# One window of destination rows for two neighbouring quads of edges

## The chip, the cores and the metric

The kernel runs on 1 core of one Trainium2 chip. The metric is the device time of one execution in microseconds (us). The engines are called by their short names: PE (TensorE), DVE (VectorE), ACT (ScalarE), POOL (GpSimd) and SP (SyncE).

## What is computed

Four graph layers run one after the other over 3125 nodes of 128 features and 53125 edges that are sorted by their destination. The change touches the first layer alone, and in it the sum over edges:

```
h = relu(layernorm(x))
msg_in = concatenate([h[src], h[dst], edge_attr])          # 128 + 128 + 2 columns
msgs = relu(msg_in @ mW1 + mb1) @ mW2 + mb2
agg = segment_sum(msgs, dst) / max(count(dst), 1)
upd = relu(concatenate([h, agg]) @ uW1 + ub1) @ uW2 + ub2 + h
x = x + layernorm(upd) * gamma + beta
```

Layers 1 to 3 are x + f(relu(layernorm(x))), where f sums the neighbours' rows (plain, weighted, or scaled by degree). The kernel does these sums as dense products with blocks of a matrix of edge counts or weights.

## The kernel before

**The sweep.** The edges are cut into 104 quads of 512 edges (NQ = 104, four chunks of 128 edges in each). One loop over the quads, called the sweep here, takes roughly from 57 us to 631 us of the profiled span. It makes the sums of layer 0 and, beside them, the count and weight blocks that the later layers use. The order of work is written out by hand, as a list of instructions and semaphore waits for each engine; nothing is scheduled by a program. For quad q:

- POOL gathers the 512 rows of the table P = h @ mW1[0:128] by the sources, as four indirect DMAs (`rows_at`, L766) into one of six buffers G. It may run six quads ahead of PE's use.
- PE makes the messages before their relu in `pre(q)`: for each chunk the identity times G (L1694) and a one-hot matrix of rows `sT` times `Qr` (L1695). `Qr` is the window of q: 125 rows of h @ mW1[128:256] from row first(q), with the two rows for the edge attributes and the bias below them. The window is one product in `q_window` on PE (L1681) into PSUM and one copy in `q_window` on DVE (L1260) to SBUF.
- ACT takes the relu (L903). PE sums the messages of the four chunks by destination in `seg(q)` (L1708), with one-hot matrices that DVE makes in `onehot` (L1266), into 128 columns of PSUM bank 2 or 3, by turns. DVE adds these to the running sums ST in `add(q)` (L1253).
- For the later layers DVE makes the operands of a step of blocks (`block_operands`, L1277, L1280, L1284), PE multiplies them in two halves, `blocks(u, 0)` and `blocks(u, 1)` (L1726, L1728), and ACT reads them (`read_blocks`, L928 and L934). Here u = q - 4.

PE's order in the loop at quad q is: pre(q + 1), blocks(u, 0), seg(q), q_window(q + 4), a piece if there is one, blocks(u, 1). ACT's is: relu(q + 1) (L903), `window_rows(q + 2)` (L916), the read of blocks(u, 0), `rows_off(q + 3)` (L909), the read of the piece of quad q - 1, the read of blocks(u, 1), normalization steps. DVE's is: add(q - 1), the window copy q + 3, the read of an A piece, onehot(q + 1), block operands, normalization steps.

**The pieces.** Where the sums of two node tiles are complete, the node update of layer 0 is done within the sweep. There are 11 such pieces g, and SLOT gives each three quads: A at 57 + 4g (sums times mW2, read by DVE, L1354), U at 59 + 4g (L1748 and L1749, relu read by ACT, L944) and V at 62 + 4g (L1755 and L1756, read by ACT, L948). The product of a piece goes into columns 256 to 511 of bank 2 or 3 (`slot_bank`), the windows into the columns between, so one bank holds a quad's sums, windows and pieces. An engine may write a bank only when no other reads it. `seg(n)` therefore waits on `s_add`, on `s_Qr` (windows copied), and on `ev[...]` for the read of the piece of slot n - 2.

After the sweep come the last piece, the layer norms of the last rows, and the dense products (L1855, L1870), which keep PE busy to the end.

Of the kernel before, what the change touches and what calls it, by code (L numbers as in the profile page):

```python
# [5 lines left out]
def gnn_kernel(nc, x_in, src_in, dst_in, ea_in, ew_in, mW1, mb1, mW2, mb2, uW1, ub1, uW2, ub2,  # L6
# [30 lines left out]
    def first(q):  # L37
        return max(0, 30 * q + (q >> 3) - 47)
# [14 lines left out]
    assert STEPS + LAG == NQ  # L53

# [8 lines left out]
    def complete(t):  # L63

        return min(q for q in range(NQ) if q + 1 == NQ or first(q + 1) >= 128 * (t + 1))
# [27 lines left out]
    with ctx:  # L93
# [95 lines left out]
        GS, QS, TS, RS, OS, OUTS, SETS = 6, 6, 4, 3, 3, 4, 3  # L189
        LEAD = 4  # L190
# [246 lines left out]
        def slot_bank(q):  # L437
            return bank(2 + q % 2)[:, 256:512]
# [408 lines left out]
        def _(act):  # L847
# [272 lines left out]
        def _(dve):  # L1120
# [47 lines left out]
            link(dve.scalar_tensor_tensor(sq[:, :], pio[:, :], 30.0, sq[:, :], ALU.mult, ALU.add))  # L1168
            link(dve.tensor_scalar(sq[:, :], sq[:, :], -47.0, 0.0, ALU.add, ALU.max))
# [70 lines left out]
            def add(q):  # L1240
                if q in SLOT:
                    name, g = SLOT[q]
                    dve.wait_ge(mm[name], g + 1)
                elif q + LEAD < NQ:
                    dve.wait_ge(s_Qmm, q + LEAD + 1)
                else:
                    dve.wait_ge(s_seg, q + 1)
                if q == 0:
                    dve.wait_ge(s_zero, 1)
                else:  # L1250
                    dve.wait_ge(s_add, q)
                at = first(q)
                dve.tensor_tensor(ST[:, at:at + 128], ST[:, at:at + 128], bank(2 + q % 2, 128), ALU.add)\  # L1253
                    .then_inc(s_add, 1)

            def q_window(n):
                dve.wait_ge(s_Qmm, max(n + 1, LEAD))
                if n >= QS:
                    dve.wait_ge(s_pre, n - QS + 1)
                dve.tensor_copy(Qr[0:WIN, n % QS, :], q_bank(n)[0:WIN, :]).then_inc(s_Qr, 1)  # L1260
# [129 lines left out]
            for n in range(LEAD):  # L1390
# [245 lines left out]
        def _(pe):  # L1636
# [42 lines left out]
            def q_window(n):  # L1679
                at = first(n)  # L1680
                pe.matmul(q_bank(n), hT[:, at:at + 128], w_m1[:, 1, :], start=True, stop=True).then_inc(s_Qmm, 1)  # L1681

            def pre(n):
# [5 lines left out]
                pe.wait_ge(s_Qr, n + 1)  # L1689
                if n >= 2:  # L1690
                    pe.wait_ge(s_R, n - 1)
                for c in range(4):
                    to = bank(n % 2)[:, 128 * c:128 * c + 128]
                    pe.matmul(to, ident[:, :], G[:, n % GS, c, :], start=True, stop=False)  # L1694
                    last = pe.matmul(to, sT[:, n % TS, 128 * c:128 * c + 128], Qr[:, n % QS, :], start=False, stop=True)  # L1695
                last.then_inc(s_pre, 1)

            def seg(n):
                pe.wait_ge(s_R, n + 1)
                pe.wait_ge(s_oh, n + 1)  # L1700
                if n >= 2:
                    pe.wait_ge(s_add, n - 1)
                pe.wait_ge(s_Qr, min(max(n - 1, 0) + LEAD, NQ))
                if n - 2 in SLOT:
                    name, g = SLOT[n - 2]
                    pe.wait_ge(ev[name], g + 1)
                for c in range(4):
                    last = pe.matmul(bank(2 + n % 2, 128), R[:, n % RS, c, :], oh[:, n % OS, c, :],  # L1708
                                     start=c == 0, stop=c == 3)
                last.then_inc(s_seg, 1)  # L1710
# [27 lines left out]
            def piece_A(g, to):  # L1738
                ts = PIECES[g]
                pe.wait_ge(s_add, complete(ts[-1]) + 1)  # L1740
# [21 lines left out]
            for n in range(LEAD):  # L1762
                q_window(n)
            pre(0)
            for q in range(NQ):
# [19 lines left out]
                if q + LEAD < NQ:  # L1785
                    q_window(q + LEAD)
# [114 lines left out]
            pe.wait_ge(s_add, NQ)  # L1901
# [101 lines left out]
```

## Time and profile before

| what | value |
|---|---|
| time, 3 runs | 1059.24 us median, 1053.53 to 1059.82 |
| span of the profiled execution, first to last instruction | 958.9 us |
| median less span (launch and end, outside the span) | 100.3 us |
| PE busy | 853.5 us (89%) |
| DVE busy | 639.7 us (67%) |
| POOL busy | 518.0 us (54%) |
| ACT busy | 509.8 us (53%) |

The profile shows one execution, and the times do not say which of the three it is. A time is therefore compared with 958.9 us plus the 100.3 us that lie outside the span. Busy shares are means over stages with different limits. Register, branch and semaphore instructions and the issue of DMAs don't count as busy, so POOL's 0.3 us between two gathers is idle time in these numbers.

### The profile page before, as it was taken

What the parts mean: (1) busy time and instruction counts of PE and PEld (TensorE: products, weight loads), DVE (VectorE), ACT (ScalarE), POOL (GpSimd) and SP (SyncE); (2) the same over time, 40 slices, a digit from 0 to 9 for tenths busy, and PEclk for the clock granted to TensorE, in tenths of its full rate; (3) what the DMA queues carried; (4) which work ended last, traced back from release to release, by engine and by line L of the source; (5) the groups of instructions that cost most, each with busy time, mean ns of one, the idle gap of its engine ahead of it and who ended that gap; (6) DMA issues with size and microseconds to landing.
All of it is one profiled execution on the core that took longest, in us unless ns stands there. A gap on an engine that the chain in (4) does not pass through costs nothing.

```text
span 958.9 us, 20995 instructions
## 1 busy us (share of the span) xinstructions
PE 853.5 (89%) x7785; PEld 783.6 (82%) x7785; DVE 639.7 (67%) x1766; ACT 509.8 (53%) x1029; POOL 518.0 (54%) x477
## 2 busy tenths in 40 slices
PE   2445988888998788999999999998999999999997
PEld 2345978888998788899998999977889888888886
DVE  7607998787877877688888889858653311115664
ACT  3413765655766556677777777843443011114863
POOL 4177777777777877777777777753110000023110
PEclk9767999999999999999999999999999999999999
DMA  5672656556765586666566666664246888884500
GB/s 153 179 176 63 180 166 177 161 171 193 209 183 166 155 148 200 170 171 182 165 184 166 172 183 167 176 194 146 69 154 232 317 287 300 299 287 144 161 23 25
DMA packets 117410, 169.14 MB, mean 176 GB/s; under 512 B 17287, under 2 KB 83485, under 8 KB 117306
## 3 DMA queue, kind: packets, MB, share of 16 engines
q1 hardware_dynamic: 99834, 137.67, 45.0%
q0 software_dynamic: 13872, 28.32, 13.4%
q10 hardware_dynamic: 3600, 1.77, 0.6%
q8 instruction: 64, 1.05, 0.5%
q14 instruction: 40, 0.33, 0.1%
HBM read 109.26 MB, written 58.45 MB: 175 GB/s over the span
## 4 chain that ended last, share of the span: by engine, by line
PE 40%; POOL 34%; issue 10%; DMA 10%; DVE 3%; ACT 2%; SPq 1%; ACTq 0%; DVEq 0%
POOL room L766 33%; PE ps L1870 14%; PE ps L1855 14%; DMA room<-p_rows,idx 7%; PE ps L1694 3%; DMA edge_windows<-room 3%; PE ps L1695 2%; PE ps L1839 2%; PE ps L1728 1%; PE ps L1708 1%; PE ps L1639 1%; ACT h L872 1%; POOL pair L766 1%; DMA ST<-in_src 1%; PE ps L1668 1%
## 5 line engine op out<-in xcount | busy, mean ns | idle before, releaser
L766 POOL DMA_INDIRECT room<-p_rows,idx x416 | 440.4, 1059 | 144.6 <-issue 120.1
L1694 PE MATMUL ps<-room,ident 128*128 128x128 f32 x832 | 175.1, 293 | 61.7 <-DMA room<-p_rows,idx 60.1
L1694 PEld LDWEIGHTS ps<-room,ident 128*128 128x128 f32 x832 | 130.9, 198 | 70.7 <-DMA room<-p_rows,idx 50.9
L1728 PE MATMUL ps<-room 128*128 128x100 bf16 x2400 | 169.3, 207 | 0.0
L1695 PE MATMUL ps<-room 128*128 128x128 f32 x832 | 166.0, 282 | 0.0
L1284 DVE TENSOR_TENSOR room<-room,Wp 128x800 bf16<-128x800 bf16 x300 | 155.4, 572 | 0.0
L903 ACT ACTIVATE g<-ps 128x512 f32<-128x512 f32 x104 | 62.2, 598 | 170.9 <-PE ps L1695 169.4
L1726 PE MATMUL ps<-room 128*128 128x100 bf16 x800 | 151.7, 208 | 0.0
L1728 PEld LDWEIGHTS ps<-room 128*128 128x128 bf16 x2400 | 147.9, 97 | 3.5
L1870 PE MATMUL ps<-room,h 128*128 128x256 f32 (+1 forms) x650 | 136.2, 371 | 0.0
L1870 PEld LDWEIGHTS ps<-room,h 128*128 128x128 f32 x650 | 119.2, 190 | 15.2
L1695 PEld LDWEIGHTS ps<-room 128*128 128x128 f32 x832 | 131.3, 199 | 0.0
L1855 PE MATMUL ps<-wide_room,parts 128*128 128x512 f32 (+1 forms) x520 | 116.7, 378 | 0.0
L1708 PE MATMUL ps<-g 128*128 128x128 f32 x832 | 116.1, 282 | 0.0
L928 ACT ACTIVATE room<-ps 128x400 uint8<-128x400 f32 x200 | 100.1, 501 | 27.8 <-PE ps L1726 26.8
L1855 PEld LDWEIGHTS ps<-wide_room,parts 128*128 128x128 f32 x520 | 91.3, 189 | 19.5 <-DVE parts L1370 0.3
L1708 PEld LDWEIGHTS ps<-g 128*128 128x128 f32 x832 | 100.8, 191 | 0.0
L934 ACT ACTIVATE room<-ps 128x400 f32<-128x400 f32 x200 | 100.7, 503 | 0.0
L1253 DVE TENSOR_TENSOR ST<-ST,ps 128x128 f32<-128x128 f32 x104 | 29.3, 282 | 104.0 <-PE ps L1681 67.4
L1266 DVE TENSOR_SCALAR g<-iota,dstT 128x128 f32<-128x128 f32 x416 | 92.1, 299 | 0.0
L864 ACT ACTIVATE sd<-mv,eps 128x2 f32<-128x2 f32 (+3 forms) x45 | 13.5, 301 | 138.0 <-DVE mv L1143 136.5
L1726 PEld LDWEIGHTS ps<-room 128*128 128x128 bf16 x800 | 78.4, 98 | 3.9 <-issue 3.6
(193 smaller groups left out, 1137.3 us busy)
## 6 DMA issues: line engine op xcount, KB each, us to landing
weight_blocks<-room SPq DMA_DIRECT2D x100, 400.0 KB
room<-weight_blocks SPq DMA_DIRECT2D x12, 3200.0 KB
room<-dst_row SPq DMA_DIRECT2D x104, 128.0 KB
room<-count_blocks SPq DMA_DIRECT2D x8, 1600.0 KB
count_blocks<-room SPq DMA_DIRECT2D x100, 100.0 KB
room<-p_rows,idx POOLq DMA_INDIRECT x416
first_c<-count_blocks SPq DMA_DIRECT2D x4, 1600.0 KB
edge_windows<-room SPq DMA_DIRECT2D x1, 3328.0 KB
```

Of the source, the lines that this page charges most:

```text
L766: return pool.indirect_dma_start(to, None, table, bass.IndirectOffsetOnAxis(ap=at, axis=0))
L928: act.activation(cnt_out[:, u % OUTS, :, at16].rearrange("p h (b w) -> p b h w", w=4), of, ACT.Copy)\
L934: act.activation(w_out[:, u % OUTS, :, at16].rearrange("p h (b w) -> p b h w", w=4), of, ACT.Copy)\
L1266: last = dve.tensor_scalar(oh[:, q % OS, c, :], iota[:, :], dstT[:, q, c:c + 1], None, ALU.is_equal)
L1284: last = dve.tensor_tensor(movw[:, k, a, :, :, :], mov[:, k, :, :, :], blocks_of(Wp[:, a, :], u, KCOLS), ALU.mult)
L1694: pe.matmul(to, ident[:, :], G[:, n % GS, c, :], start=True, stop=False)
L1695: last = pe.matmul(to, sT[:, n % TS, 128 * c:128 * c + 128], Qr[:, n % QS, :], start=False, stop=True)
L1708: last = pe.matmul(bank(2 + n % 2, 128), R[:, n % RS, c, :], oh[:, n % OS, c, :], start=c == 0, stop=c == 3)
L1726: counted = pe.matmul(bank(4 + hh)[:, at], lo, mov[:, k, i, :, t], start=True, stop=True)
L1728: weighed = pe.matmul(bank(6 + hh)[:, at], lo, movw[:, k, a, i, :, t], start=a == 0, stop=a == PARTS - 1)
L1855: last = pe.matmul(to, Hr[:, t, a, :], at[:, k, 0:n], start=a == 0 and t == 0, stop=a == 1 and t == NT - 1)
L1870: last = pe.matmul(bank(dense_bank(j))[:, 256 * half:256 * half + 32 * c], h[:, t, :], ring_w[(2 * j + half) % 3][:, 0:c, t, :], start=t = ...
```

## The change

Quads 2m and 2m + 1 form a pair. Both use the same first row: first(q) is max(0, 30 (q & ~1) + (q >> 3) - 32) where it was max(0, 30 q + (q >> 3) - 47). So there is one window product and one copy for a pair (52 instead of 104, two pairs ahead, 4 buffers Qr for pairs instead of 6 for quads), and seg(2m) and seg(2m + 1) accumulate into the same 128 columns, from which DVE adds once for a pair. The banks alternate by pairs. A window is written after seg of an even quad, into the bank that the pair does not use; ahead of it stands the new wait `other_bank_free(n)`, on the add of the pair before and, if quad n - 1 was the slot of a piece, on the read of that piece. seg(n) keeps its waits on windows and pieces for even n alone.

```diff
     def first(q):
-        return max(0, 30 * q + (q >> 3) - 47)
+        return max(0, 30 * (q & ~1) + (q >> 3) - 32)
...
         def q_bank(n):
-            at = 256 if 2 <= n < LEAD else 128
-            return bank(2 + n % 2)[:, at:at + 128]
+            return bank(2 + (n + 1) % 2)[:, 128:256]
...
         def slot_bank(q):
-            return bank(2 + q % 2)[:, 256:512]
+
+            m = q // 2 if q % 2 else q // 2 + 1
+            return bank(2 + m % 2)[:, 256:512]
...
@@ ACT, read_slot
-                act.wait_ge(s_add, q + 1)
-                if q + LEAD < NQ:
-                    act.wait_ge(s_Qr, q + LEAD + 1)
+                if q % 2:
+                    act.wait_ge(s_add, q // 2 + 1)
+                elif q // 2 + AHEAD < NH:
+                    act.wait_ge(s_Qr, q // 2 + AHEAD + 1)
...
@@ DVE, the loop
                 if q >= 1:
-                    add(q - 1)
-                    if q - 1 + LEAD < NQ:
-                        q_window(q - 1 + LEAD)
+                    if (q - 1) % 2:
+                        add(q // 2 - 1)
+                    elif q // 2 + AHEAD < NH:
+                        q_window(q // 2 + AHEAD)
...
@@ PE
             def seg(n):
+                m = n // 2
                 pe.wait_ge(s_R, n + 1)
                 pe.wait_ge(s_oh, n + 1)
-                if n >= 2:
-                    pe.wait_ge(s_add, n - 1)
-                pe.wait_ge(s_Qr, min(max(n - 1, 0) + LEAD, NQ))
-                if n - 2 in SLOT:
-                    name, g = SLOT[n - 2]
+                if n % 2 == 0:
+                    pe.wait_ge(s_Qr, min(m + AHEAD, NH))
+                    if n - 2 in SLOT:
+                        name, g = SLOT[n - 2]
+                        pe.wait_ge(ev[name], g + 1)
+                for c in range(4):
+                    last = pe.matmul(bank(2 + m % 2, 128), R[:, n % RS, c, :], oh[:, n % OS, c, :],
+                                     start=n % 2 == 0 and c == 0, stop=n % 2 == 1 and c == 3)
+                last.then_inc(s_seg, 1)
+
+            def other_bank_free(n):
+
+                pe.wait_ge(s_add, n // 2)
+                if n - 1 in SLOT:
+                    name, g = SLOT[n - 1]
                     pe.wait_ge(ev[name], g + 1)
...
                 seg(q)
-                if q + LEAD < NQ:
-                    q_window(q + LEAD)
+                if q % 2 == 0:
+                    if q >= 2:
+                        other_bank_free(q)
+                    else:
+                        pe.wait_ge(s_Qr, AHEAD)
+                    if q // 2 + AHEAD < NH:
+                        q_window(q // 2 + AHEAD)
```

The other hunks adapt counts to this (the semaphore values of `add`, `pre` and `piece_A`, one more small instruction on DVE that makes first(q) for every partition, two rows of constants less to load for each Qr buffer that is gone).

PE at quad 68, the quad after slot U of piece 2, before: seg (L1708), window (L1681), second half of the blocks. Names after "waits" are semaphores.

```order
L1708 MATMUL ps<-g3 128x128 [waits q_window_ready,quad_added,V_read,onehot_ready,messages_ready]
L1708 MATMUL ps<-g3 128x128 x3
L1681 MATMUL ps<-w_m1,hT 128x128
L1726 MATMUL ps<-room 128x100 [waits weights_read,counts_read]
L1728 MATMUL ps<-room 128x100 x3
```

The same place after the change (seg is L1718 there, the window L1691):

```order
L1718 MATMUL ps<-g3 128x128 [waits q_window_ready,V_read,onehot_ready,messages_ready]
L1718 MATMUL ps<-g3 128x128 x3
L1691 MATMUL ps<-w_m1,hT 128x128 [waits U_read,quad_added]
L1743 MATMUL ps<-room 128x100 [waits weights_read,counts_read]
L1745 MATMUL ps<-room 128x100 x3
```

The wait for the reading of the U piece has moved from seg of quad 69 (not shown) to the window of quad 68, and the wait for the add from ahead of seg to behind it.

ACT at the same quad, before: relu, window rows, the blocks' first half, rows off, the read of the U piece (L944).

```order
L903 ACTIVATE g3<-ps 128x512 [waits quad_in_psum,messages_in_psum]
L916 ACTIVATE room<-room,onesr 125x512 [waits messages_in_psum,rows_off_ready]
L928 ACTIVATE room<-ps 128x4x25x4 [waits counts_stored_0,counts_in_psum]
L934 ACTIVATE room<-ps 128x4x25x4 [waits weights_stored_0,weights_in_psum]
L909 ACTIVATE room<-room,npio 125x512 [waits dst_spread_3]
L944 ACTIVATE ST<-ps,cols 128x256 [waits U_done,q_window_ready,quad_added]
```

And after:

```order
L906 ACTIVATE g3<-ps 128x512 [waits quad_in_psum,messages_in_psum]
L919 ACTIVATE room<-room,onesr 125x512 [waits messages_in_psum,rows_off_ready]
L931 ACTIVATE room<-ps 128x4x25x4 [waits counts_stored_0,counts_in_psum]
L937 ACTIVATE room<-ps 128x4x25x4 [waits weights_stored_0,weights_in_psum]
L912 ACTIVATE room<-room,npio 125x512 [waits dst_spread_3]
L947 ACTIVATE ST<-ps,cols 128x256 [waits U_done,quad_added]
```

Nothing moved on ACT; one wait of the read of the piece is gone.

## Rows read from the trace of the kernel before

**Rows 1.** Waits over the whole span: us in total, times, longest.

```profile
POOL room L766 <- issue: 120.1, 394, 0.3
...
PE ps L1694 <- DMA room<-p_rows,idx: 60.1, 43, 17.7
...
POOL room L766 <- PE ps L1695: 6.4, 21, 0.3
```

**Rows 2.** Waits between 400 and 626 us.

```profile
POOL room L766 <- issue: 47.0, 154, 0.3
...
PE ps L1694 <- DMA room<-p_rows,idx: 7.7, 10, 1.6
```

**Rows 3.** Source view of the gathers L766: duration min/median/max in ns, first and last start.

```profile
L766 POOL DMA_INDIRECT room<-p_rows,idx x416: 939/947/4158, 45.2 to 619.9; - x139
```

**Rows 4.** Timeline at 439 us, POOL and DVE: start, us, engine, line.

```profile
439.21 0.95 POOL L766 DMA_INDIRECT room<-p_rows,idx  x1 [0.30 <-issue]
439.24 0.29 DVE L1253 TENSOR_TENSOR ST<-ST,ps 128x128 f32<-128x128 f32 x1 [0.89 <-PE ps L1749]
439.44 0.28 DVE L1260 COPY room<-ps 125x128 f32<-125x128 f32 x1
440.43 0.56 DVE L1277 TENSOR_TENSOR room<-iota_k,Kt 128x800 bf16<-128x800 bf16 x1
440.46 1.35 POOL L766 DMA_INDIRECT room<-p_rows,idx  x1 [0.30 <-issue]
```

**Rows 5.** Timeline of PE at quad 68.

```profile
443.30 0.39 PE L1681 MATMUL ps<-w_m,hT 128*128 128x128 f32 x2
443.53 0.21 PE L1726 MATMUL ps<-room 128*128 128x100 bf16 x1
```

**Rows 6.** Timeline of ACT at quad 68.

```profile
441.82 0.60 ACT L903 ACTIVATE g<-ps 128x512 f32<-128x512 f32 x1 [0.33 <-PE ps L1695]
...
444.31 0.48 ACT L944 ACTIVATE ST<-ps,cols 128x256 f32<-128x256 f32 x1
```

**Rows 7.** Timeline at quad 96, the last but one of its kind.

```profile
595.75 0.39 PE L1681 MATMUL ps<-w_m,hT 128*128 128x128 f32 x2
...
596.75 0.48 ACT L944 ACTIVATE ST<-ps,cols 128x256 f32<-128x256 f32 x1
```

**Rows 8.** PE's first and last wait of [rows 2], of ten.

```profile
402.05 0.49 PE L1694 MATMUL ps<-room,ident 128*128 128x128 f32 x2 [0.96 <-DMA room<-p_rows,idx]
...
624.42 0.49 PE L1694 MATMUL ps<-room,ident 128*128 128x128 f32 x2 [1.59 <-DMA room<-p_rows,idx]
```

**Rows 9.** DVE's read of an A piece (quad 74), PE's window.

```profile
472.74 0.41 DVE L1354 TENSOR_TENSOR room<-ps,room 128x256 f32<-128x256 f32 x1
...
476.51 0.39 PE L1681 MATMUL ps<-w_m,hT 128*128 128x128 f32 x2
```

**Rows 10.** Timeline at quad 4, PE and DVE, and the next wait of PE for a gather.

```profile
97.35 0.39 PE L1681 MATMUL ps<-w_m,hT 128*128 128x128 f32 x2
98.63 0.27 DVE L1253 TENSOR_TENSOR ST<-ST,ps 128x128 f32<-128x128 f32 x1
...
122.71 0.49 PE L1694 MATMUL ps<-room,ident 128*128 128x128 f32 x2 [1.81 <-DMA room<-p_rows,idx]
```

**Rows 11.** Chain that ended last, 619 to 642 us: start, us, what.

```profile
619.92 4.45 DMA room<-p_rows,idx
...
641.71 0.49 ACT h L948
```

**Rows 12.** PE after a longer wait; windows (the third number from the end is the granted clock).

```profile
237.17 0.49 PE L1694 MATMUL ps<-room,ident 128*128 128x128 f32 x2 [1.98 <-DMA room<-p_rows,idx]
...
238.00:240.00 2.00, 2.00 (x12) 2.00 (x11) 0.48 (x1) 0.00 (x0) 1.39 (x3) 0.50 1.10 344
240.00:242.00 2.00, 2.00 (x24) 1.94 (x24) 0.00 (x0) 1.38 (x3) 1.70 (x2) 0.75 1.11 366
...
124.00:126.00 2.00, 2.00 (x29) 1.99 (x29) 2.00 (x5) 1.21 (x3) 1.59 (x2) 1.00 0.68 151
```

More of the change, by code:

```diff
@@ L53, in gnn_kernel @@
     assert STEPS + LAG == NQ
+    NH = NQ // 2
+    AHEAD = 2
+    assert NQ == 2 * NH
     PIECES = [[t, t + 1] for t in range(0, NT - 3, 2)] + [list(range(NT - 3, NT))]
@@ L63, in complete @@
     def complete(t):
-        return min(q for q in range(NQ) if q + 1 == NQ or first(q + 1) >= 128 * (t + 1))
+        return min(q for q in range(1, NQ, 2) if q + 1 == NQ or first(q + 1) >= 128 * (t + 1))
     SLOT = {}
@@ L1167, in _ @@
             link(dve.tensor_copy(sq[:, :], q8_i[:, :]))
-            link(dve.scalar_tensor_tensor(sq[:, :], pio[:, :], 30.0, sq[:, :], ALU.mult, ALU.add))
-            link(dve.tensor_scalar(sq[:, :], sq[:, :], -47.0, 0.0, ALU.add, ALU.max))
+            link(dve.tensor_single_scalar(q8_i[:, :], pio_i[:, :], 126, ALU.bitwise_and))
+            link(dve.scalar_tensor_tensor(sq[:, :], q8_i[:, :], 30.0, sq[:, :], ALU.mult, ALU.add))
+            link(dve.tensor_scalar(sq[:, :], sq[:, :], -32.0, 0.0, ALU.add, ALU.max))
             dve.wait_ge(s_dst, 48)
@@ L1238, in _, with add @@
             dve.memset(ST[:, :], 0.0).then_inc(s_zero, 1)
-            def add(q):
+            def add(m):
+                q = 2 * m + 1
                 if q in SLOT:
@@ L1388, in piece_steps @@
                         stage(g)
-            for n in range(LEAD):
+            for n in range(AHEAD):
                 q_window(n)
@@ L1679, in q_window @@
             def q_window(n):
-                at = first(n)
+                at = first(2 * n)
                 pe.matmul(q_bank(n), hT[:, at:at + 128], w_m1[:, 1, :], start=True, stop=True).then_inc(s_Qmm, 1)
@@ L1688, in pre @@
                 pe.wait_ge(s_sT, n + 1)
-                pe.wait_ge(s_Qr, n + 1)
+                pe.wait_ge(s_Qr, n // 2 + 1)
                 if n >= 2:
@@ L1694, in pre @@
                     pe.matmul(to, ident[:, :], G[:, n % GS, c, :], start=True, stop=False)
-                    last = pe.matmul(to, sT[:, n % TS, 128 * c:128 * c + 128], Qr[:, n % QS, :], start=False, stop=True)
+                    last = pe.matmul(to, sT[:, n % TS, 128 * c:128 * c + 128], Qr[:, n // 2 % QS, :], start=False, stop=True)
                 last.then_inc(s_pre, 1)
             def seg(n):
+                m = n // 2
                 pe.wait_ge(s_R, n + 1)
                 pe.wait_ge(s_oh, n + 1)
-                if n >= 2:
-                    pe.wait_ge(s_add, n - 1)
-                pe.wait_ge(s_Qr, min(max(n - 1, 0) + LEAD, NQ))
-                if n - 2 in SLOT:
-                    name, g = SLOT[n - 2]
+                if n % 2 == 0:
[11 more added lines that the diff above has]
+                    name, g = SLOT[n - 1]
                     pe.wait_ge(ev[name], g + 1)
[L1707 to L1710, printed above, removed]
             def blocks(u, hh):
@@ L1739, in piece_A @@
                 ts = PIECES[g]
-                pe.wait_ge(s_add, complete(ts[-1]) + 1)
+                pe.wait_ge(s_add, complete(ts[-1]) // 2 + 1)
                 pe.wait_ge(s_ld[g % RING], 32 * (g // 3 + 1))
@@ L1761, in _ @@
             pe.wait_ge(s_edE, 2)
-            for n in range(LEAD):
+            for n in range(AHEAD):
                 q_window(n)
@@ L1784, in _ @@
                 seg(q)
-                if q + LEAD < NQ:
-                    q_window(q + LEAD)
+                if q % 2 == 0:
+                    if q >= 2:
+                        other_bank_free(q)
+                    else:
+                        pe.wait_ge(s_Qr, AHEAD)
+                    if q // 2 + AHEAD < NH:
+                        q_window(q // 2 + AHEAD)
                 if q in SLOT:
@@ L1900, in _ @@
             dense_group(1, 0)
-            pe.wait_ge(s_add, NQ)
+            pe.wait_ge(s_add, NH)
             pe.wait_ge(ev["V"], IN_SWEEP)
```

19 lines of the change are left out of this document (10 added, 9 removed).

## The prediction

> **What bounds the kernel now.** The totals mislead here. PE is busy for 89% of the span, but in the sweep it waits for POOL. I read the waits first. Over the whole span POOL's idle time before a gather is almost all "issue", 0.3 us at a time, and its waits for PE's `pre` are never longer than that same 0.3 us [rows 1]: POOL never waits for a free buffer once the gathers run. A gather takes 0.947 us at the median [rows 3] and 0.30 us lies between two, so four gathers, a quad, cost at least 5.0 us, and the 416 of them set the sweep's pace. PE on the other hand has waited 60.1 us for gathered rows [rows 1].
>
> The reader is then to see how this changes along the sweep. Between 400 and 626 us, where the pieces are made, PE's waits for gathers sum to only 7.7 us in ten waits [rows 2], of 0.96 us at the first and 1.59 us at the last [rows 8], while POOL goes on without a pause. There PE and POOL are nearly even: POOL is ahead by 7.7 us in 226, 3.4%. Whatever is taken from PE gains nothing; whatever is added to it costs nothing up to those 7.7 us, and after that the whole amount. At the end the chain goes from the last gather (619.92) through its landing into PE at 624.42 and on, without a wait for another engine, to ACT at 641.71 [rows 11]. So how late PE is at its last gather arrives in full at the end.
>
> **The windows and adds that go.** 52 of 104 window products leave PE. One costs PE 0.23 us, from the window's start at 443.30 to the next product at 443.53 [rows 5]. That is 12.0 us over the sweep, but up to quad 59 it only lengthens PE's waits for gathers. DVE loses 52 adds (0.29 us) and 52 copies (0.28 us) [rows 4], 30 us in all. DVE is not what POOL or, in steady state, PE waits for, so this is worth nothing by itself. Could a lighter DVE speed the gathers? A gather that runs beside an add and a copy takes 0.95 us, the median; one that starts beside the block operands L1277 takes 1.35 us [rows 4]. What slows gathers is left as it was. I take 0 for it. The bound on the good side is that each of the 52 adds and copies held up a gather for its whole length, 30 us, which the 0.95 us speaks against.
>
> **The new waits on the add.** After seg(2m) PE now waits for add(m - 1), which DVE does at the head of its turn 2m. Before the change PE needed DVE one turn less far. In steady state DVE stands ready early. It is late only at the start, behind the unpacking of the windows: at quad 4 the add of quad 3 ends at 98.63 + 0.27 = 98.90, and PE is through seg at 97.35 [rows 10], so PE would wait 1.6 us; the same at quad 6 is some 0.4 us. Behind the waiting window on PE stand the second half of the blocks and the next `pre`. POOL is several quads ahead at this point and has six buffers, and PE's next wait for a gather at 122.71 is 1.81 us long [rows 10]. Together with DVE's shorter turns that covers it: 0, and if the cover failed, 2 us in a stretch that is followed by 280 us in which POOL is ahead.
>
> **The new waits on pieces.** A slot's read was waited for by seg two quads later. Now it is waited for one quad later, by the window (or, from quad 100 on, by the blocks behind it). For A pieces this is free: DVE starts its read at 472.74 and needs 0.41 us, and PE comes to the window of that quad only at 476.51 [rows 9]. V pieces stand at even quads and keep their wait. For U pieces it is not free. ACT starts its turn with the relu at 441.82, just after PE's `pre` of the same turn, and comes to L944 only after four other instructions, at 444.31; it ends at 444.79 [rows 6]. PE is through seg at 443.30 [rows 5]. PE now stands for 444.79 - 443.30 = 1.49 us and a few hundredths for the semaphore, say 1.53 us. Both engines start from the same product, so this is the same each time: at quad 96 it is 596.75 + 0.48 - 595.75 = 1.48 us [rows 7]. ACT doesn't start earlier after the change, since its order is the same and its start hangs on PE. There are 11 U pieces (slots 59 to 99), so 16.8 us are added to PE between 400 us and the end. Queued behind the wait are the window, the blocks' second half and the next `pre`, for which ACT and DVE then wait in turn; DVE's copy of the window comes 1.5 us later and its add in the next turn stood idle for longer than a microsecond, so DVE absorbs this.
>
> **The sum.** From quad 60 on, PE gains 16.8 us of standing and loses 20 of 40 windows, 4.6 us: 12.2 us more. 7.7 us of its waits for gathers take up the first part. A wait can only take up lateness that is there when it comes; the first stall, at 400 us, precedes the first wait of 0.96 us, and each group of four quads then adds 1.53 - 2 x 0.23 = 1.07 us of lateness against some 0.7 us of waiting (7.7 / 11), so all 7.7 us are used. PE is late at its last gather by 12.2 - 7.7 = 4.5 us. This goes through the chain to the end. 958.9 + 4.5 = 963.4 us of span, and with the 100.3 us outside it 1063.7 us, or 0.4% more than the median of 1059.24. Lateness of 4.5 us is less than one quad of the six that POOL may run ahead, so POOL is not held up.
>
> **Rivals.** *Not slower: the stalls are hidden.* If PE's own pace had more room than its waits show (waits under 0.3 us are not in the list), or if DVE's shorter turns and a steadier PE bring ACT's turn forward, up to the whole of 4.5 us disappears. Some 0.4 us more room for each group of four quads is enough. POOL alone then sets the end, 1059 us. For it speaks that PE and POOL are so nearly even that small errors decide; against it that the 1.48 us repeats to the hundredth in [rows 5 to 7].
>
> *Slower by much: the clock drops at the stalls.* After PE's wait of 1.98 us the granted clock stood at 0.50 for 2 us and at 0.75 for 2 us more [rows 12], the lower of its two levels (1.2 GHz of 2.4) for part of the time; that lost 1.0 + 0.5 = 1.5 us. After the wait of 1.81 us at 122.71 it stayed at 1.00 [rows 10, 12]. A stall of 1.5 us lies just under these. If it decided the clock each time, 11 x 1.5 = 16.5 us would come on top: 1080 us. [...] The Trainium skill ("TensorE: Matmul & The Clock Gate", section "Why this matters for your kernels") would allow idle gaps longer than any of these before the clock falls back; by it this rival has no ground. The trace disagrees, with a drop after 1.98 us, so I keep it.
>
> *The gathers change their pace.* What a gather loses to DVE's block operands depends on how the two fall together; 1.35 against 0.95 us is 0.4 us for an unlucky one [rows 4]. DVE's turns are now 0.29 us shorter, so all meetings shift. One gather in each quad that meets or misses would be 0.4 x 50 = 20 us over the first 50 quads at the most, either way; a tenth to a third of the meetings is what I would expect, 2 to 6 us: 1058 to 1070 us. Once PE is the bound, from quad 64 or so, a faster POOL gains nothing. The Trainium skill ("SBUF — State Buffer", section on who interferes with whom) says that VectorE instructions in a two-port mode hold a port that GpSimd needs to write descriptors. Were the window's copy one of these, as the page says of fp32 copies within SBUF, its removal would give up to 52 x 0.28 = 15 us; the 0.95 us beside it speaks against that.
>
> *The change doesn't do what it says.* If some quad's destinations fell outside 125 rows, the kernel would redo everything in its slow branch, for milliseconds. A pair covers some 60 rows of destinations plus the drift, so 65 are left. 1%.
>
> **How the numbers follow.** Chances: forecast (1061 to 1067) 0.55; stalls hidden 0.15; pace of the gathers, 0.08 for faster (1045 to 1058) and 0.11 for slower (1067 to 1075) than the others give; clock 0.08 (1080); anything else 0.03. The range of 1054 to 1073 leaves out the clock and the ends of the pace. One per cent is 10.6 us, about what a measurement of this kernel can tell from no change: the three runs before lie 6.3 us apart. Within 1% (1048.6 to 1069.8) lie the forecast, the hidden stalls and most of the pace: 0.80. Slower by more: the clock and part of the pace, 0.15. Faster by more: 0.05.
>
> **What the profile after should show.** PE waits of 1.4 to 1.6 us at the window L1691 for ACT L947, ten of them, and one more at the blocks of quad 100. PE's waits for gathers after 405 us gone or nearly so, and the last `pre` starting about 4 us after its gather has landed, at about 629 us. POOL's gathers unchanged, 416 with a median of 0.947 us and the last one at about 620 us. 52 each of L1257, L1269 and L1691. Up to 400 us more waiting of PE for gathers, by about the windows that went. If the last gather itself ends earlier or later by more than 3 us, the pace has changed and the sum is made from a wrong base. If PE still waits for its last gather, the stalls were hidden. If the granted clock after 400 us falls below 1.00, it is the clock.

## The result and the profile after

The changed kernel takes 1086.15 us at the median of four runs (1084.93 to 1091.63), the kernel before 1059.53 us at the median of four (1053.53 to 1062.10): a ratio of 1.0278, with a 95% interval of 1.0245 to 1.0311. It is slower by 27 us where 4.5 us were forecast, outside the range and on the side that got 0.15.

The profiled execution took 1086.68 us and its span is 1082.7 us. So only 4 us lie outside the span, where [rows 1 to 12] came from an execution with a span 100 us under the time. The waits over the whole span, in the order us in total, times, longest:

```profile
POOL room L769 <- issue: 99.4, 325, 0.4
...
POOL room L769 <- PE ps L1705: 81.9, 40, 5.4
...
POOL room L769 <- remote: 65.7, 50, 2.4
...
PE ps L1745 <- issue: 45.2, 82, 1.2
```

This is not the kernel of [rows 1]. POOL, which waited for PE 0.3 us at a time there, now waits 5.4 us at the longest, and PE stands 82 times at the products of the weight blocks (L1745) without any semaphore. PE's stalls at the window L1691 behind the U slots 59, 63 and so on are all there; four of the ten and the one at quad 100 from PE's timeline:

```profile
467.93 0.77 PE L1691 MATMUL ps<-w_m,hT 128*128 128x128 f32 x2 [2.57 <-issue]
...
551.82 0.56 PE L1691 MATMUL ps<-w_m,hT 128*128 128x128 f32 x2 [3.03 <-ACT ST L947]
...
607.26 0.77 PE L1691 MATMUL ps<-w_m,hT 128*128 128x128 f32 x2 [3.19 <-issue]
...
719.06 0.55 PE L1691 MATMUL ps<-w_m,hT 128*128 128x128 f32 x2 [3.17 <-ACT ST L947]
...
742.74 0.21 PE L1743 MATMUL ps<-room 128*128 128x100 bf16 x1 [1.42 <-issue]
```

The ten last 30.1 us together (2.44 to 3.21 each), twice what was forecast. PE's last product of counts in the turn before the stall at 719.06, and ACT up to that stall:

```profile
711.09 0.20 PE L1743 MATMUL ps<-room 128*128 128x100 bf16 x1
...
714.40 0.51 ACT L931 ACTIVATE room<-ps 128x400 uint8<-128x400 f32 x1 [2.37 <-remote]
714.80 0.50 ACT L937 ACTIVATE room<-ps 128x400 f32<-128x400 f32 x1
715.19 0.87 ACT L875 ACTIVATE h<-x,nb,rs 128x128 f32<-128x128 f32 x2
715.96 0.59 ACT L906 ACTIVATE g<-ps 128x512 f32<-128x512 f32 x1
...
718.43 0.49 ACT L947 ACTIVATE ST<-ps,cols 128x256 f32<-128x256 f32 x1
```

From the start of the relu to the end of the U read ACT needs 718.43 + 0.49 - 715.96 = 2.96 us, as in [rows 6], where it is 2.97. What differs is where the relu stands against PE. PE's `seg` ended at 719.06 - 3.17 = 715.89, so the relu starts with the end of `seg`; in [rows 5, 6] it started 1.48 us ahead of it. Ahead of the relu stands ACT's read of the blocks, held for 2.37 us. What it waits for is PE's product of 711.09, which ends at 711.30; the trace also has the times at which semaphores are incremented, by which one engine tells another that an instruction is done (no line above prints them), and the increment of this product arrives only at 714.38.

The stall does not end in PE. POOL's gathers around the one at 607.26:

```profile
603.05 0.99 POOL L769 DMA_INDIRECT room<-p_rows,idx  x1 [1.38 <-PE ps L1705]
604.35 0.94 POOL L769 DMA_INDIRECT room<-p_rows,idx  x1 [0.30 <-issue]
605.59 0.94 POOL L769 DMA_INDIRECT room<-p_rows,idx  x1 [0.30 <-issue]
606.84 0.95 POOL L769 DMA_INDIRECT room<-p_rows,idx  x1 [0.30 <-issue]
613.18 0.94 POOL L769 DMA_INDIRECT room<-p_rows,idx  x1 [5.40 <-PE ps L1705]
```

POOL waits for PE in every quad, 1.4 us, and 5.40 us in the one behind the stall: here the gathers start some 4 us later than their pace asks. The stall itself was 3.19 us. From the first gather of quad 66 to that of quad 103, nine of POOL's steps from quad to quad lie behind a stall and take 82.7 us; the others take 6.21 us each, so a stall cost 3.0 us at the mean. How that comes about is told under "Why the prediction was wrong".

### The profile page after: what moved, and what is told of

It is laid out like the page before. It is cut to its first block, busy times and chain, and to the rows that moved or that the text cites. A ratio compares the mean times of both kernels' runs of the same rounds, so it can differ in the third digit from the quotient of the medians.

```text
span 1082.7 us, 20507 instructions
## 1 busy us (share of the span) xinstructions
PE 887.9 (82%) x7681; PEld 796.8 (74%) x7681; DVE 631.5 (58%) x1663; ACT 514.3 (48%) x1029; POOL 499.2 (46%) x477
## 4 chain that ended last, share of the span: by engine, by line
PE 78%; issue 12%; ACT 3%; DVE 3%; another core or an unknown queue 1%; DMA 1%; POOL 1%; SPq 0%; ACTq 0%; DVEq 0%
PE ps L1892 12%; PE ps L1745 12%; PE ps L1877 12%; PE ps L1704 10%; PE ps L1718 10%; PE ps L1705 9%; PE ps L1743 4%; PE ps L1861 2%; PE ps L1691 2%; ACT h L875 1%; DMA room<-p_rows,idx 1%; PE ps L1649 1%; PE ps L1760 1%; POOL room L769 1%
## 5 line engine op out<-in xcount | busy, mean ns | idle before, releaser
L769 POOL DMA_INDIRECT room<-p_rows,idx x416 | 421.7, 1014 | 258.5 <-issue 99.4
L1745 PE MATMUL ps<-room 128*128 128x100 bf16 x2400 | 194.2, 211 | 47.2 <-issue 45.2
L1704 PE MATMUL ps<-room,ident 128*128 128x128 f32 x832 | 179.0, 299 | 37.9 <-DMA room<-p_rows,idx 16.3
L1745 PEld LDWEIGHTS ps<-room 128*128 128x128 bf16 x2400 | 155.7, 100 | 62.2 <-issue 57.7
L1705 PE MATMUL ps<-room 128*128 128x128 f32 x832 | 171.0, 289 | 0.1
L1743 PE MATMUL ps<-room 128*128 128x100 bf16 x800 | 157.9, 212 | 12.4 <-issue 12.1
L1704 PEld LDWEIGHTS ps<-room,ident 128*128 128x128 f32 x832 | 136.8, 206 | 42.2 <-issue 39.0
L1718 PE MATMUL ps<-g 128*128 128x128 f32 x832 | 125.9, 287 | 16.5 <-issue 15.5
L1705 PEld LDWEIGHTS ps<-room 128*128 128x128 f32 x832 | 136.0, 206 | 0.0
L1286 DVE TENSOR_TENSOR room<-iota_k,Kt 128x800 bf16<-128x800 bf16 x100 | 57.4, 574 | 133.0 <-remote 128.0
L1718 PEld LDWEIGHTS ps<-g 128*128 128x128 f32 x832 | 105.6, 193 | 24.2 <-issue 23.8
L1743 PEld LDWEIGHTS ps<-room 128*128 128x128 bf16 x800 | 80.4, 101 | 20.4 <-issue 19.9
```

Of the source, the lines that this page charges most:

```text
L769: return pool.indirect_dma_start(to, None, table, bass.IndirectOffsetOnAxis(ap=at, axis=0))
L1718: last = pe.matmul(bank(2 + m % 2, 128), R[:, n % RS, c, :], oh[:, n % OS, c, :], start=n % 2 == 0 and c == 0, stop=n % 2 == 1 and c == 3)
L1743: counted = pe.matmul(bank(4 + hh)[:, at], lo, mov[:, k, i, :, t], start=True, stop=True)
L1745: weighed = pe.matmul(bank(6 + hh)[:, at], lo, movw[:, k, a, i, :, t], start=a == 0, stop=a == PARTS - 1)
```

## The experiments

Times of the same kernel differ from one set of runs to the next (before: 1059 and 1072 us, and on one chip 1071.54 and later 1058.53), so each kernel is set against the runs of before in its own set.

**The kernel before once more, and the ranges alone.** *b_same* is the unchanged kernel; *p1_range* has only `first(q)` and `complete(t)` of the change:

```diff
-        return max(0, 30 * q + (q >> 3) - 47)
+        return max(0, 30 * (q & ~1) + (q >> 3) - 32)
```

> The kernel before, unchanged, profiled again beside the changed one. The page of before has a span of 958.9 us against a time of 1059 us, the page of after 1082.7 us against 1086 us. If the profiled execution of before was one in an unusual state (theory A), this span is near 1055 us, 4 us below its time, with PE standing without a semaphore ('issue') in the sweep as in the profile after. If the change itself brought these stalls (theory B), the span is 959 us again, without them, and 100 us lie outside it.

> One part alone: the row ranges of the pairs (both quads of a pair use the same first row), but with a window product, a copy and an add for every quad as before. It computes the same output. Every theory that blames waits, windows or adds expects the time of before, 1059 us within 5. If the ranges themselves cost (consecutive adds to the same columns of ST, or pieces becoming complete later), it goes towards 1086 us.

One run each, beside 1071.54 us of before: 1075.62 us (span 1073.8) and 1073.85 us (span 1072.0). The ranges cost nothing that one run can show. *b_same* is as theory A had it: the span is near the time, and PE stands without a semaphore in the kernel before too. Its waits over the whole span:

```profile
ACT room L928 <- remote: 235.6, 90, 5.8
...
POOL room L766 <- remote: 77.6, 50, 5.7
PE ps L1728 <- issue: 68.7, 129, 1.2
POOL room L766 <- PE ps L1695: 68.0, 40, 4.8
...
PE ps L1694 <- DMA room<-p_rows,idx: 19.0, 1, 19.0
```

The unchanged kernel waits for a gather once, at the start, where [rows 1] has 43 such waits and 60.1 us. It is POOL that waits for PE. From quad 8 to 44 a quad lasts 6.255 us between ACT's relus, against 5.342 in the execution of [rows 1 to 12]. Every later trace has a span within 4 us of the time and stands of PE in the sweep (short ones in *e4_gathers*): [rows 1 to 12] describe an execution that the timed ones are not. Why that one ran otherwise no run shows. Its timeline at 301 us, PE, ACT and POOL:

```profile
300.92 0.39 PE L1695 MATMUL ps<-room 128*128 128x128 f32 x2
...
301.31 1.15 POOL L766 DMA_INDIRECT room<-p_rows,idx  x1 [0.30 <-issue]
...
302.55 0.21 PE L1728 MATMUL ps<-room 128*128 128x100 bf16 x1 [0.50 <-issue]
...
303.27 0.21 PE L1726 MATMUL ps<-room 128*128 128x100 bf16 x1 [0.52 <-issue]
...
303.32 0.51 ACT L928 ACTIVATE room<-ps 128x400 uint8<-128x400 f32 x1 [2.86 <-remote]
...
303.76 0.94 POOL L766 DMA_INDIRECT room<-p_rows,idx  x1 [1.30 <-remote]
```

Once per quad PE slows down or stops inside the blocks, with no semaphore to wait for. The last gather ahead of POOL's pause ends at 301.31 + 1.15 = 302.46, PE is at full pace again at 303.27, 0.81 us later, and ACT and POOL are released behind it. From 200 to 630 us POOL pauses for over 0.6 us 63 times; in 58 of them PE's last resumption within the pause lies 0.79 to 1.04 us behind the gather's end.

The times of the increments say what is held. POOL's gather at 303.76 waits for PE's `pre`, whose last product ends at 301.31. Its increment arrives at 303.51. At the median of 59 quads from 200 to 600 us it arrives 2.13 us behind the end of `pre` and 1.25 us behind the end of POOL's last gather, and POOL goes on 0.26 us later. In the same stretch the increments of ACT and DVE arrive 0.01 us behind their instructions. So do all 95 recorded ones of PE after 770 us, where no gather runs, and all of PE in the execution of [rows 1 to 12]. PE's work is thus not what POOL waits for, as far as its recorded ends go (they are modelled): PE has room, 2 us in most quads and 1 to 2 us from quad 64 on, where the pieces are.

**The wait for the U read alone, and three versions without it.** *e2_wait* is the kernel before with only the moved wait:

```diff
                 seg(q)
+                if SLOT.get(q - 1, " ")[0] == "U":
+                    pe.wait_ge(ev["U"], SLOT[q - 1][1] + 1)
                 if q + LEAD < NQ:
```

> The kernel before with one thing added: PE's window of the quad after each U slot waits until ACT has read the U piece, as in the changed kernel. The output is the same. T1: 11 stalls of about 3 us, 30 us or more slower than before (1085 to 1095). T2: at most the 4.5 us that the prediction worked out, about 1064 us.

*e1_defer* is the changed kernel, with the window behind a U slot, its wait and its copy one quad later:

```diff
-                if q % 2 == 0:
+                if q % 2 == 0 and not after_U(q):
...
+                if after_U(q - 1):
+                    other_bank_free(q - 1)
+                    if q // 2 + AHEAD < NH:
+                        q_window(q // 2 + AHEAD)
```

> The changed kernel, but behind a U slot the window and its wait stand one quad later on PE, as do the copy on DVE; the output is the same. Theory T1 (the wait of the window for ACT's read of the U piece, 3.15 us in each of 11 groups, makes the change slow): these stalls go, the clock dips behind them too, and what is left is the gain from 52 fewer windows and adds; 31 us less than the changed kernel, so 1050 to 1056 us where before is at 1059. Rival T2 (sums over two quads in one bank, with banks that alternate every two quads, hold PE up by themselves): still 1080 us or more.

*e3_early_read* is the changed kernel, with ACT's U read right behind the relu of the same turn:

```diff
                 if q + 1 < NQ:
                     relu(q + 1)
+                if SLOT.get(q - 1, " ")[0] == "U":
+                    read_slot(q - 1)
```

> The changed kernel, with ACT reading a U piece right after the relu of the same turn instead of behind four more instructions; PE's order and waits are those of the changed kernel. T1: the stall ends some 2 us earlier, so it shrinks from 3.15 us to about 1 us or less; 1055 to 1068 us. T2: no change, 1086 us.

*p2_window* shares window and copy in a pair, but sums, adds and waits per quad as before:

```diff
-                if q + LEAD < NQ:
-                    q_window(q + LEAD)
+                if q + LEAD < NQ and q % 2 == 0:
+                    q_window((q + LEAD) // 2)
```

> One part alone: ranges and window products and copies for pairs, but sums, adds and all waits per quad as before; the output is the same. By the pace that the traces show in quads 8 to 60 (7.3 us gained by the whole change in 52 quads), PE is limited by what it issues, and 52 windows less on PE give 8 to 14 us: 1046 to 1052 us. If POOL's gathers set the pace, as the prediction had it: 1059 us, no change.

| kernel | median us | ratio to before, 95% interval | ACT's relus of quads 60 to 100, us |
|---|---|---|---|
| changed | 1086.15 | 1.0278, 1.0245 to 1.0311 | 275.9 |
| e2_wait | 1089.80 | 1.0286, 1.0262 to 1.0310 | 276.1 |
| e1_defer | 1055.11 | 0.9965, 0.9943 to 0.9988 | 246.2 |
| e3_early_read | 1057.90 | 0.9986, 0.9956 to 1.0016 | 246.7 |
| p2_window | 1055.42 | 0.9966, 0.9948 to 0.9985 | 246.2 |

The last column is read from ACT's timeline of each profiled execution. The one wait in the kernel before makes the whole loss, and each way of removing it from the changed kernel removes the whole loss, 275.9 - 246.2 = 29.7 us from quad 60 to 100. The ten stalls last 30.1 us; that the two agree is chance, as shown further down. The rival (pair sums and banks cost something themselves) falls with *e1_defer* and *e3_early_read*. PE in *e2_wait* at the same slots:

```profile
471.58 0.79 PE L1681 MATMUL ps<-w_m,hT 128*128 128x128 f32 x2 [2.39 <-issue]
...
554.21 0.79 PE L1681 MATMUL ps<-w_m,hT 128*128 128x128 f32 x2 [3.04 <-ACT ST L944]
```

*e1_defer* beats both kernels: 1059.94 - 1055.11 = 4.8 us less than before (the interval of the ratio allows 1.3 to 6.0). *p2_window* has the same ratio, so all the gain is the 52 windows and their copies; summing a pair together adds nothing that these runs can tell. Its 1055.42 us lie between the two times of its expectation (1046 to 1052 if PE's issue were the limit, 1059 if the gathers were). *e3_early_read*'s interval includes 1, so it can't be told from before.

*e6_both* puts both repairs together. 

> The changed kernel with both repairs: behind a U slot the window and its wait stand one quad later on PE, and ACT reads the U piece right behind the relu of the same turn. If the wait for the U read was the whole loss, each repair alone removes it and the second has nothing left to give: 0.995 to 0.999 of before, as the first repair alone (0.9965). If ACT's earlier read also frees something on the way (V pieces wait for U), it would go below 0.994.

1064.76 us against 1072.97, ratio 0.9947 (0.9916 to 0.9979): a hair under the range of 0.995 to 0.999 and above the 0.994 of the other case. The interval overlaps that of *e1_defer*, so no gain of the second repair is shown.

**Who sets the pace?** By now I took PE for the bound, since POOL waited for it. Two kernels asked. *e4_gathers* is the kernel before without every fourth gather:

```diff
-                for c in range(4):
+                for c in range(3):
                     rows_at(G[:, q % GS, c, :], P_tab, idx[:, q, c:c + 1]).then_inc(s_gat[q % GS], 16)
...
-                    pe.matmul(to, ident[:, :], G[:, n % GS, c, :], start=True, stop=False)
+                    pe.matmul(to, ident[:, :], G[:, n % GS, c % 3, :], start=True, stop=False)
```

> The kernel before, with 312 gathers in place of 416: the fourth gather of every quad is left out, and PE multiplies the third chunk's rows in its place, so PE, ACT and DVE issue what they did (the messages of every fourth chunk are computed from the wrong rows). If POOL's gathers set the sweep's pace, as the prediction's first step had it, a quad can go from four gathers (5.0 us and more) to three (3.75 us) and PE's waits for gathers, 60.1 us in the page of before, go away: the time falls by 40 to 60 us. If PE is the bound in timed executions, where it stood for a gather once in the trace of the unchanged kernel (19.0 us at the start), nothing changes once the sweep runs: ratio 0.99 to 1.00, with POOL's waits for PE up by 104 x 1.25 = 130 us.

*e5_products* is the kernel before without PE's third weight product:

```diff
-                    for a in range(PARTS):
+                    for a in range(PARTS - 1):
```

> The kernel before, with PE's third product of each weight block left out (8 of some 58 products of a quad; the weights of the later layers lose their last part, DVE still makes its operand, ACT reads as before). If PE is the bound, each of the 8 products gives back its place in the row, 116.2 us / 1428 = 0.081 us, so 0.65 us of 6.25 in a quad and 65 us over 100 quads: 990 to 1010 us, unless ACT or DVE comes to the front before that. If POOL sets the pace, the same time as before, with PE waiting 0.6 us more in each quad. The stand of 1.2 us that PE makes once in some 58 products without a semaphore should also move: if it comes by the count of products it comes every 1.15 quads, if by the quad (something that ACT, DVE or POOL does) still once in each.

*e4_gathers* took 946.33 us against 1072.97, ratio 0.8806 (0.8763 to 0.8849): 126.6 us less, 1.22 us for each of the 104 gathers. *e5_products* took 1064.97 us, ratio 0.9927 (0.9897 to 0.9956): 8 us less, not 65 (and not 0, which the other case had; where the 8 come from is open). So PE as the bound was wrong on both, and the other case, the gathers, was sized too small in *e4_gathers* (40 to 60 us). The gathers set the pace after all, although PE never waits for one. *e4_gathers* at the same place as above, PE and POOL:

```profile
300.32 0.95 POOL L766 DMA_INDIRECT room<-p_rows,idx  x1 [0.30 <-issue]
...
301.72 0.21 PE L1726 MATMUL ps<-room 128*128 128x100 bf16 x1
302.08 0.31 PE L1728 MATMUL ps<-room 128*128 128x100 bf16 x3 [0.15 <-issue]
...
302.61 1.00 POOL L766 DMA_INDIRECT room<-p_rows,idx  x1 [1.34 <-PE ps L1695]
```

The gather ahead of POOL's pause ended at 300.32 + 0.95 = 301.27 and PE is back 0.81 us later, as in *b_same*, but it stood for 0.15 us instead of over 1. A quad lasts 4.95 us (quads 8 to 44) against 6.255: a gather with its gap (0.95 + 0.30 us) less, with the pause left as it was.

The increments of `pre` show why both came out so. In *e5_products* they arrive 2.57 us behind the end of `pre` at the median, since PE is done earlier, but 1.14 us behind the last gather; in *e4_gathers* 0.42 us behind `pre`, since PE has less time, and 1.11 us behind the last gather. Against the last gather they stay where they are, 1.1 to 1.25 us, whatever PE does. POOL's next four gathers wait for them.

**A pause for POOL.** From this came a reading, called H: while POOL issues gathers back to back, PE is held, and let go 0.8 to 1.0 us after the last of them; POOL in turn needs PE's next `pre`. A quad then lasts four gathers and the pause, 5.0 + 1.25 us, as long as PE's own work in it is less. *e7_pause* (before) and *e8_pause_after* (changed) add

```diff
+                    if c == 1:
+                        link(pool.memset(idle[:, :], 0.0))
+                        link(pool.memset(idle[:, :], 0.0))
```

> The kernel before, with a pause on POOL between the second and the third gather of every quad: two small memsets of a tile that nobody reads, some 1.0 us (computation unchanged). Reading H (formed from the traces of the unchanged kernel and of e4_gathers): while POOL issues gathers back to back, PE comes to a stand without a semaphore and goes on 0.8 to 1.0 us after the end of the last gather before POOL pauses, so a quad lasts the four gathers (5.0 us) and 1.25 us of standing. With a pause in the middle, PE is let go there, 0.8 to 1.0 us after the second gather, and needs only 4.6 us of its own work for a quad; POOL's waits for PE (1.3 to 1.5 us in each quad) go, and a quad lasts 5.0 us and the pause, 6.0 to 6.2 us: 1035 to 1065 us, not slower, although POOL has 104 us more to do. Rival: PE's stand goes with the number of gathers or their bytes, not with POOL's pauses. Then the pause is added to each quad, 6.25 + 1.0 us, or 1130 to 1165 us, or if the pause falls into POOL's wait for PE, the time is the same but PE's stands stay behind the fourth gather as before.

> The changed kernel with the same pause on POOL between the second and the third gather of every quad. By H ACT's turn is no longer held until the end of the four gathers, so PE's stand for ACT's U read falls from 3.15 us to about the 1.5 us that the prediction read, and since PE then has 1 us or more to spare in each quad (6.0 to 6.2 of pace against 4.6 of work), most of it is caught up: within 1% of e7_pause, where the change without the pause lost 2.8%. If the size of the stall and its full price do not come from the held releases, PE stands 3.0 us or more ten times again and the kernel is 20 to 30 us slower than e7_pause.

*e7_pause* took 1070.65 us against 1058.53, ratio 1.0103 (1.0068 to 1.0139). Its timeline, POOL and PE:

```profile
304.36 0.94 POOL L767 DMA_INDIRECT room<-p_rows,idx  x1 [0.30 <-issue]
...
305.30 0.43 POOL L781 MEMSET idle<- 128x384 bf16 x1
...
305.79 0.42 POOL L782 MEMSET idle<- 128x384 bf16 x1
306.11 0.25 PE L1732 MATMUL ps<-room 128*128 128x100 bf16 x2 [1.12 <-issue]
...
306.48 1.06 POOL L767 DMA_INDIRECT room<-p_rows,idx  x1 [0.27 <-POOL idle L782]
```

The gather ends at 305.30 and PE is back at 306.11, 0.81 us later: the resumption has moved to POOL's new pause. 104 pauses of 306.48 - 305.30 = 1.18 us, or 123 us, cost 12.1 us. POOL's waits for PE, 68.0 and 77.6 us in *b_same*, are no longer among its waits of over 20 us. This bears H out in place, and against its rival (1130 to 1165 us); the time lies 6 us over the range I gave, with a quad of 6.65 us for 6.0 to 6.2 (quads 8 to 44), and why is open.

*e8_pause_after* took 1084.57 us, ratio 1.0269 (1.0213 to 1.0326), 13.9 us more than *e7_pause*. That is 1.3%, between the two cases that I had set out (within 1%, or 20 to 30 us). H's expectation on the stalls failed: the ten sum to 35.3 us, not 15. One of them:

```profile
602.87 0.60 ACT L910 ACTIVATE g<-ps 128x512 f32<-128x512 f32 x1
...
605.82 0.50 ACT L935 ACTIVATE room<-ps 128x400 uint8<-128x400 f32 x1 [1.74 <-remote]
...
607.21 0.47 ACT L951 ACTIVATE ST<-ps,cols 128x256 f32<-128x256 f32 x1
607.83 0.77 PE L1695 MATMUL ps<-w_m,hT 128*128 128x128 f32 x2 [4.27 <-ACT ST L951]
```

The relu is early now (602.87), but ACT is held for 1.74 us behind it, at the read of the blocks. The hold had moved from ahead of the relu into the stretch between relu and U read, so the U read is no earlier. Quads 60 to 100 take 283.5 us between ACT's relus, against 259.9 in *e7_pause*: 23.6 us for 35.3 us of stalls, where the changed kernel without the pause has 29.7 for 30.1. Up to quad 60 it is the faster one (332.3 us from quad 8 to 60 against 339.6), which makes the difference of the times smaller. A pause at just any place does not shorten the stall.

## Why the prediction was wrong, by its steps

**What bounds the kernel: right in name, wrong in what follows.** The step said that four gathers a quad set the pace, and that PE had 7.7 us to spare. *e4_gathers* confirms the first half. But the 7.7 us came from [rows 2, 8], and in the timed executions PE has no wait for gathers to fill: POOL is six quads ahead and waits in each quad for the increment of PE's `pre`, which comes late. PE's room is larger than 7.7 us there, and it is of another kind. The hint was there in the small table: 100.3 us outside the span.

**Windows and adds: right in size.** 4.6 us were expected from the windows from quad 60 on, and nothing from the adds. *e1_defer* gives 4.8 us over the whole sweep, *p2_window* without the pair sums the same. That it comes from quad 60 on alone is not shown: neither set has a trace of before. The gathers' durations stayed at a median of 945 ns (947 in [rows 3]).

**New waits on the add, on A and V pieces: right.** Between 400 and 750 us no stand of PE in *e1_defer*, where these waits remain, is longer than 1.14 us, and none of over 0.6 us is at a window.

**The U wait: right place and count, half the size.** This is the first term that failed: "PE now stands for ... 1.53 us" and "Both engines start from the same product, so this is the same each time". It measured 3.01 us at the mean of ten (30.1 / 10). ACT's own 2.96 us were right to 0.01. Its start was not bound to PE's product alone, as the step had it, but to the reads ahead of the relu, and these wait for increments of PE that arrive late: 3.08 us behind the product at the stall of 719.06 (714.38 - 711.30).

**The clock: put outside the sum, and it was in the time.** This is the second term that failed. The rival stood at 0.08, because a stall of 1.5 us "lies just under" the waits after which the clock had moved. The stalls were of 3 us, and at or just behind each of the ten the granted clock fell to 0.50 for 3.4 or 6.8 us. PE in three windows of 6 us (the third number from the end is the granted clock), the first and third from a stall on, the second between stalls:

```profile
466.00:472.00 6.00, 4.08 (x28) 4.04 (x29) 3.64 (x11) 2.68 (x7) 2.60 (x3) 0.56 0.51 143
484.00:490.00 6.00, 5.40 (x62) 4.88 (x61) 4.72 (x15) 3.67 (x8) 3.69 (x4) 1.00 0.43 139
496.00:502.00 6.00, 6.00 (x57) 5.92 (x58) 4.05 (x12) 2.73 (x7) 2.24 (x2) 0.72 0.47 141
```

Two stalls of nearly one length show its price. Behind the one at 579.56 the clock is back before the end of `pre`, behind the one at 607.26 it is not:

```profile
579.14 0.94 POOL L769 DMA_INDIRECT room<-p_rows,idx  x1 [0.30 <-issue]
579.56 0.77 PE L1691 MATMUL ps<-w_m,hT 128*128 128x128 f32 x2 [3.15 <-issue]
...
583.71 0.39 PE L1705 MATMUL ps<-room 128*128 128x128 f32 x2
...
584.37 0.94 POOL L769 DMA_INDIRECT room<-p_rows,idx  x1 [4.29 <-PE ps L1705]
...
612.28 0.63 PE L1705 MATMUL ps<-room 128*128 128x128 f32 x2
```

The granted clock in a stretch of 3 us at each place (again the third number from the end):

```profile
582.80:585.80 3.00, 3.00 (x37) 2.99 (x36) 2.22 (x7) 1.70 (x5) 1.12 (x2) 1.00 0.65 210
610.30:613.30 3.00, 3.00 (x21) 2.94 (x20) 2.43 (x7) 0.59 (x2) 0.12 (x1) 0.50 0.77 202
```

From the window to the end of `pre` PE takes 583.71 + 0.39 - 579.56 = 4.54 us and 612.28 + 0.63 - 607.26 = 5.65 us, where at a clock of 1.00 it takes 2.97 us (304.60 to 307.57 in *b_same*). POOL's wait grows by the same 1.11 us, from 4.29 to 5.40, for a stall that is 0.04 us longer. Over the ten stalls these stretches sum to 48.5 us against 29.7, so the clock cost PE 18.8 us on the way to POOL. In *e2_wait* two stalls of ten have the long stretch (5.67 and 5.68 us), and POOL's steps behind them are 10.07 us against 8.3 to 9.1 behind the seven others that a gather follows. The rival's 16.5 us and its 1080 us were near, for a stall twice the one that it was worked out for. The page of the Trainium skill that the prediction set against this rival ("TensorE: Matmul & The Clock Gate", section "Why this matters for your kernels") disagrees with the windows behind the stalls of 2.57 and 2.44 us, as it did with [rows 12]; eight of the ten stalls are longer than the gap of some 3 us that it names.

**The full price of a stall, and the sum.** 16.8 - 4.6 - 7.7 = 4.5 us were forecast. Measured are 30.1 us of stalls at the windows, 1.4 at quad 100, 18.8 of the clock and 4.8 less of windows, 45.5 us, where the time shows 26.6 (1086.15 - 1059.53). So some 19 us of lateness were taken up, 1.9 for each stall, and not 7.7 in all. This fits the room that PE has: in *e1_defer* the increment of the same `pre` (quads 62, 66 and so on) arrives 1.3 to 2.1 us behind its end, so a `pre` later by that much delays nothing. That the loss equals the sum of the stalls is chance, since what the clock added is what the room took up. What is left is passed on in full: PE's `pre` lets POOL start the next four gathers, and they set the pace, so POOL's later steps (6.15, 6.23 and 6.22 us behind the stall of 607.26) win nothing back. The terms of clock and room are read from traces; no run has all these stalls at a clock of 1.00. One stall of *e8_pause_after* has it, 2.33 us before 687.72: there the stretch to the end of `pre` takes 3.04 us.

**The other rivals.** *Hidden stalls* fell: each cost 3.0 us. *The gathers change their pace* fell too: their median stayed (945 ns for 947), and the four that follow each other without a wait still take 5.0 us.

**Open.** Why PE's increments arrive late in the sweep, and whether the work behind them is late too or only the word of it. That gathers back to back are not enough for it is shown by the execution of [rows 1 to 12], which had them for the whole sweep and no late increment; why, no run shows. The loading of instructions is not it by its count: the pages of that execution and of *b_same* both have 64 packets in the queue "q8 instruction", for 104 quads.

## What to carry to other kernels

Compare the span of a profile with the time first: where 100 us lie outside it, take another profile before using its waits as slack. When a wait for a buffer moves one step earlier, look who reads the buffer and where that read stands in the reader's order; moving the writer back by one quad cost a few lines and turned 2.8% lost into 0.35% gained, and moving the read up behind the relu brought it back to the time of before. When a stall is read from a trace, look at the granted clock of the work behind it before its price is written down, and at the room that the engine has: two terms of 19 us cancelled here. And read the bound from what a removed instruction gives back, not from who waits for whom: POOL waited for PE here, and yet a gather less was worth 1.22 us and eight PE products less in a quad 0.08 us.

## What the runs showed of the hardware

In every trace of the sweep but that of [rows 1 to 12], PE's semaphore increments arrive late while POOL issues indirect DMAs (0.95 us each, 0.30 us apart): for `pre` 2.13 us behind the recorded end at the median of *b_same*, against 0.01 us for ACT and DVE there, and 0.01 us for PE where no gather runs. They come 1.1 to 1.25 us behind the end of the last DMA ahead of POOL's pause in *b_same*, *e4_gathers* and *e5_products*. PE stands or crawls in the same time with no semaphore to wait for, and is at full pace again 0.79 to 1.04 us after that DMA (58 of 63 pauses of *b_same*). ACT, DVE and POOL, where they wait for PE, are released only then; ACT's wait that ended at 303.32 was 2.86 us long. Not every release follows so soon: at the start of the sweep, with 35 such DMAs in a row in *b_same*, DVE went on 5.6 us behind the last of them (93.40). Of its 50 us of waiting 22.7 lie behind the recorded end of PE's `seg` (76.30); up to there PE had not done the work.

```profile
92.46 0.94 POOL L766 DMA_INDIRECT room<-p_rows,idx  x1 [0.30 <-issue]
...
99.03 0.29 DVE L1253 TENSOR_TENSOR ST<-ST,ps 128x128 f32<-128x128 f32 x1 [50.10 <-remote]
99.13 0.94 POOL L766 DMA_INDIRECT room<-p_rows,idx  x1 [5.73 <-remote]
```
